# A fused two-layer graph kernel: z one step and o one step earlier, TensorE's order h, o, z, and the seventh batch's open o units done ahead of the last batch's z

## The reference, cut to what matters

```python
# layer 0: four Gaussian kernels on the relation weights, only their row sums are needed
w = exp(-0.5 * (adj[..., None] - mean) ** 2 / (1e-14 + prec ** 2))
ws = sum(w / sum(w, axis=-1), axis=2)                 # b, row, kernel
x1 = layernorm(x + concat_n(ws[n] * (x @ W[n].T)))
# layer 1: one expert per batch, chosen by the mean of x1
top1 = argmax(x1.mean(axis=1) @ router_w + router_b)
out = adj @ (x1 @ expert_w[top1])
y = relu(batchnorm_over_the_batches_of_one_expert(out))
result = layernorm(x1 + y)
```

## Time and profile before

| | us |
|---|---|
| median of 3 runs | 908.11 |
| profiled execution | 911.44 |
| its span | 909.7 |
| TensorE (PE) busy | 754.8 (83%) |
| VectorE (DVE) busy | 761.7 (84%) |
| ScalarE (ACT) busy | 772.7 (85%) |
| GpSimd (POOL) busy | 693.6 (76%) |

### The profile page before, as it was taken

How to read it: one execution, slowest core, us unless ns; L and a number is a source line. 1 busy time by engine, 2 the same in 40 slices (tenths; PEclk the granted TensorE clock), 3 DMA queues, 4 the chain that set the end, 5 groups by cost and what they waited for, 6 DMA issues and landing times.

```text
span 909.7 us, 12461 instructions
## 1 busy us (share of the span) xinstructions
PE 754.8 (83%) x3922; PEld 354.9 (39%) x3922; DVE 761.7 (84%) x1636; ACT 772.7 (85%) x761; POOL 693.6 (76%) x788
## 2 busy tenths in 40 slices
PE   1544458799999999999999999999999989994650
PEld 1211123344444444444444444444444434443640
DVE  1999988979999999999999999999999932327991
ACT  5999989989999999999999999999999811118971
POOL 6699999998888888888888888888888220002996
PEclk9866669899999999999999999999999999998895
DMA  8789887887797879877877798889766200898997
GB/s 231 206 256 254 208 225 175 211 196 197 197 239 193 190 183 239 205 190 187 232 186 187 194 243 198 194 199 234 186 163 162 47 1 0 314 359 318 333 391 284
DMA packets 262677, 191.18 MB, mean 210 GB/s; under 512 B 210002, under 2 KB 210258, under 8 KB 261074
## 3 DMA queue, kind: packets, MB, share of 16 engines
q1 hardware_dynamic: 262466, 190.38, 76.9%
q10 hardware_dynamic: 144, 0.00, 0.0%
HBM read 91.52 MB, written 48.50 MB: 154 GB/s over the span
## 4 chain that ended last, share of the span: by engine, by line
DVE 45%; POOL 22%; ACT 14%; PE 10%; issue 5%; DMA 2%; SPq 0%; DVEq 0%; POOLq 0%; ACTq 0%
DVE wgt L825 17%; DVE ps_t L857 17%; DVE x_in L844 5%; PE ps_z L1012 5%; ACT ps_t L593 4%; ACT ps_t L591 4%; POOL adj_cut L453 4%; PE ps_o L1028 3%; POOL adj_in L448 2%; POOL x_turn L464 2%; POOL x1p L490 2%; POOL adj_cut L451 2%; PE ps_t L1028 2%; POOL adjT L548 2%; DMA w_sel<-w_planes 1%
## 5 line engine op out<-in xcount | busy, mean ns | idle before, releaser
L1012 PE MATMUL ps_z<-adjT,x1p 128*128 128x512 f16 x1536 | 345.0, 381 | 0.0
L997 PE MATMUL ps_h<-w0T,x_turn 128*128 128x512 f16 x768 | 195.5, 409 | 74.0 <-DVE x_in L844 55.9
L857 DVE TENSOR_TENSOR ps_t<-ps_t,wgt 128x1024 f32<-128x1024 f32 x192 | 235.9, 1229 | 22.4 <-ACT ps_t L587 17.8
L825 DVE SCALAR_TENSOR_TENSOR wgt<-wgt,ps_t 128x1024 f32<-128x1024 f32 x192 | 224.8, 1215 | 17.4 <-ACT ps_t L593 17.2
L1012 PEld LDWEIGHTS ps_z<-adjT,x1p 128*128 128x128 f16 x1536 | 150.3, 98 | 181.6 <-issue 4.6
L576 ACT ACTIVATE wgt<-adj_in,neg_mu 128x1024 f32<-128x1024 f32 x192 | 205.8, 1136 | 8.2 <-POOL adj_in L448 8.2
L582 ACT ACTIVATE wgt<-wgt 128x3072 f32<-128x3072 f32 x64 | 176.5, 2758 | 0.0
L1028 PE MATMUL ps_o<-zT,w_sel 128*128 128x512 f16 x684 | 159.4, 383 | 6.7 <-DMA w_sel<-w_planes 6.6
L997 PEld LDWEIGHTS ps_h<-w0T,x_turn 128*128 128x128 f16 x768 | 75.8, 103 | 183.6 <-issue 95.6
L453 POOL TENSOR_TENSOR adj_cut<-adj_in,adj_cut 128x1024 f16<-128x1024 f32 x64 | 136.6, 2134 | 5.3
L1028 PEld LDWEIGHTS ps_o<-zT,w_sel 128*128 128x128 f16 x684 | 67.1, 99 | 89.8 <-DMA w_sel<-w_planes 8.5
(11 more groups left out here) (219 smaller groups left out, 859.8 us busy)
## 6 DMA issues: line engine op xcount, KB each, us to landing
adj_in<-in_adj_dram SPq DMA_DIRECT2D x64, 512.0 KB, 4.0
x_in<-in_x_dram SPq DMA_DIRECT2D x64, 256.0 KB, 4.3
x_spill<-x_in SPq DMA_DIRECT2D x28, 512.0 KB, 3.3
out_spill<-o_stage SPq DMA_DIRECT2D x49, 256.0 KB, 2.9
w_sel<-w_planes SPq DMA_DIRECT2D x8, 1024.0 KB, 5.9
adjT<-x_spill SPq DMA_DIRECT2D x6, 1024.0 KB, 12.6
out_dram<-adjT SPq DMA_DIRECT2D x6, 1024.0 KB, 7.2
adjT<-out_spill SPq DMA_DIRECT2D x4, 1024.0 KB, 13.1
```

The lines of the kernel that those rows point to most:

```text
L825: v.scalar_tensor_tensor(out=wgt[:, m % 2, j, :], in0=wgt[:, m % 2, j, :], scalar=SUM_SCALE / W0_SCALE, in1=tot, op0=ALU.mult, op1=ALU.mul ...
L857: v.tensor_tensor(tot, tot, wgt[:, n % 2, j, :], ALU.add).then_inc(dve_tot, 1)
L997: last = te.matmul(ps_h[:, n % 2, :], xT[:, n % 2, left, c, :], w0T[:, right, c, :], start=(c + i == 0), stop=(c == C - 1 and i == 2))
L1012: last = te.matmul(ps_z[:, u % 2, :], x1p[:, b % 2, left, t, k * P:(k + 1) * P], adjT[:, b % 2, right, t, half * HALF:(half + 1) * HALF], ...
```

## The change

`Z_LAG` goes from 10 to 9 and `O_LAG` from 14 to 13, so `LAST` falls from 80 to 79 and `KEPT` (from which unit on o stays on the chip) rises from 49 to 50. TensorE's step becomes h, o, z; ScalarE copies o before z. At step 65 (`FLUSH`) the four open o units of the seventh batch, 52 to 55, are all done before z(56), and at step 64 z stands ahead of o; steps 66 to 68 have no o. z(8b) waits for the x1 tiles one by one and for only the four turned tiles of adj that its half reads; the second sum for the router follows it. SyncE stores the experts' planes ahead of the transposes of steps 3, 5, 7 and 9 instead of at their ends, and the last step fetches two chunks of half a row of o instead of one.

```diff
-Z_LAG = 10
-O_LAG = 14
+Z_LAG = 9
+O_LAG = 13
...
+        FLUSH = TILES - T + Z_LAG
+        def z_unit(n):
+            return range(max(0, n - Z_LAG), min(TILES, n - Z_LAG + 1))
+        def o_units(n):
+            u = n - O_LAG
+            if n == FLUSH:
+                return range(u, TILES - T)
+            if FLUSH < n < TILES - T + O_LAG:
+                return range(0)
+            return range(max(0, u), min(TILES, u + 1))
+        def z_ahead_of_o(n):
+            return n == FLUSH - 1
...
@@ SyncE
+                if n in (3, 5, 7, 9):
+                    e = (n - 3) // 2
+                    sp.wait_ge(dve_wlo, 2 * e + 2)
+                    sp.dma_start(w_planes[e]..., planes(e)).then_inc(planes_stored, 16)
                 if n + 1 < TILES:
                     turn_adj(n + 1)
...
@@ ScalarE, step n (take_z and take_o hold the copies as before)
+                if z_ahead_of_o(n - 1):
+                    take_z(n - 1)
+                take_o(n - 1)
+                if not z_ahead_of_o(n - 1):
+                    take_z(n - 1)
                 if 0 <= n - 1 < TILES:
                     sum_reciprocal(n - 1)
...
@@ TensorE, z_product(u)
-                if u % T == 0:
-                    pe.wait_ge(pool_1l, u + T)
-                    mean(b, 1).then_inc(pe_mean, 1)
+                if k == 0:
                     for j in range(2):
-                        pe.wait_ge(adj_turned[j], 16 * (u + T) // 2)
+                        pe.wait_ge(adj_turned[j], 16 * (u + G) // 2)
                 wait(pe, dve_z, u - 1)
                 for t in range(T):
+                    if u % T == 0:
+                        pe.wait_ge(pool_1l, u + t + 1)
...
+                if u % T == 0:
+                    mean(b, 1).then_inc(pe_mean, 1)
...
@@ TensorE, step n
-                if 0 <= n - Z_LAG < TILES:
-                    z_product(n - Z_LAG)
-                if 0 <= n - O_LAG < TILES:
-                    o_product(n - O_LAG)
+                if z_ahead_of_o(n):
+                    for u in z_unit(n):
+                        z_product(u)
+                for u in o_units(n):
+                    o_product(u)
+                if not z_ahead_of_o(n):
+                    for u in z_unit(n):
+                        z_product(u)
```

More of the change, by code:

```diff
@@ L366, in fetch_o @@
                 if n == 1:
-                    sp.wait_ge(o_stored[0], KEPT // 2 * 16 + 16)
                     sp.wait_ge(dve_ws, NK * (TILES - 1))
-                    for half in (slice(0, HALF // 2), slice(HALF // 2, HALF)):
-                        sp.dma_start(o_chunk(i, 0)[:, half], out_spill[b, 0:P, half]).then_inc(o_back[i], 16)
+                    for k in range(2):
+                        sp.wait_ge(o_stored[k], KEPT // 2 * 16)
+                        sp.dma_start(o_chunk(i, k)[:, 0:HALF], out_spill[b, k * P:(k + 1) * P, 0:HALF]).then_inc(o_back[i], 16)
                 elif 1 < n < NB:
@@ L593, in sum_reciprocal, with take_z, take_o @@
                 s.activation(tot, tot, ACT.Exp, scale=-1.0).then_inc(act_rec, 1)
+            def take_z(n):
+                for u in z_unit(n):
+                    half, k = u % T // G, u % G
+                    act.wait_ge(pe_z, u + 1)
+                    if k == 0:
+                        wait(act, pe_o, u - G)
+                    if u == 0:
+                        act.wait_ge(planes_stored, 16 * E)
+                    s.activation(zT[:, 0, half, k, :], ps_z[:, u % 2, :], ACT.Copy,
+                                 scale=Z_SCALE / (ADJ_SCALE * X1_SCALE)).then_inc(act_z, 1)
+            def take_o(n):
+                for u in o_units(n):
+                    k = u % G
+                    act.wait_ge(pe_o, u + 1)
+                    if u >= KEPT:
+                        act.wait_ge(dve_ws, NK * (TILES if u // T == NB - 1 else TILES - 1))
+                        for j in range(2):
+                            act.wait_ge(adj_turned[j], 16 * TILES // 2)
+                    else:
+                        wait(act, o_stored[k % 2], u // 2 * 16)
+                        wait(act, dve_ostat, u - 1)
+                    if u == TILES - 1:
+                        act.wait_ge(dve_ostat, TILES)
+                    s.activation(out_unit(u), ps_out(u), ACT.Copy).then_inc(act_o, 1)
             for n in range(LAST):
@@ L861, in _ @@
                     y_stats(n - 2)
-                if 0 <= n - Z_LAG - 1 < TILES:
-                    low_z(n - Z_LAG - 1)
+                for u in z_unit(n - 1):
+                    low_z(u)
                 if 0 <= n - 2 < TILES:
                     y_mean_var(n - 2)
-                if 0 <= n - O_LAG - 1 < TILES:
-                    o_stats(n - O_LAG - 1)
+                for u in o_units(n - 1):
+                    o_stats(u)
                 if 1 <= n <= 2 * E:
```

33 lines of the change are left out of this document (5 added, 28 removed).

## The result

The changed kernel takes 934.79 us (median of 4 runs, 931.64 to 936.9) against 909.6 us for the kernel before on the same chip (906.81 to 911.09): ratio 1.0281, 95% interval 1.0243 to 1.0319, so it is slower. The profiled execution took 936.9 us, its span is 935.1, that is 25.4 more than before.

A forecast was written before the change was run, and what follows sets the result against it. ScalarE and VectorE were taken to bound the main part, then TensorE alone its tail. Seven delays +21.0, start +1.2 and tail -3.5 gave +18.7 us, 926.8 us on the median, range 911 to 937.

The forecast's parts named there:

- the fifth case: Rival for the whole kernel: slow landing and 2.4 us for the clock each time, +33 us, 941 us; chance 0.07.
- The wait for `w_sel` in front of z: TensorE at the first o of batches 0 to 6: seven idle times of 4 to 5 us, slow clock behind them.
- Its size: Main part, each of seven gaps: the step 3.0 us longer, 21.0 us in all; bounds for one 0.1 to 4.7.
- The landing term: Load of w_sel in the main part: lands 5.9 us after its issue (median, 4.8 to 7.0).
- The clock: TensorE's work behind each long gap runs at the slow clock, 1.8 us extra on average.
- The cause behind it: Main part: w_sel can't be asked for before the routing has chosen the expert, and only h covers its flight.
- The second case: Rival: the waits for w_sel are there but TensorE's clock stays high, +4.3 us, 912.4 us; chance 0.13.
- The third: Rival: w_sel comes in time, main part as before, the tail loses 15.5 us, 892.6 us; chance 0.09.
- The fourth: Rival: quick landings (about 5.0), gap short enough for the clock in most batches, -2 us, 906 us; chance 0.09.
- The start: First batch: ScalarE's step 10 waits for z(0), +4.7 us; the first o's stall of 3.5 goes; net +1.2.
- ScalarE's copy: Each step 8b+14: ScalarE's copy of z waits 2 to 4 us for TensorE; batch spacing grows from 88 to about 91.
- The tail: TensorE's stretch after the main part: 3.5 us shorter, no wait for x1, one of about 4 us for w_sel.

The follow-up runs named there:

- Experiment 1: The changed kernel with z ahead of o also in the step of every batch's first o: 905.82 us, ratio 0.9963 to the kernel before.
- experiment 2: The changed kernel with 18 unread matmuls on TensorE between h and the first o of batches 0 to 6: 921.05 us, ratio 1.0145 to the kernel before.
- experiment 10: The changed kernel with the old lags 10 and 14, order h, o, z and flush kept: 928.8 us, ratio 1.0233 to the kernel before.
- experiment 9: The changed kernel with old lags 10 and 14 and old order h, z, o, flush kept: 901.12 us, ratio 0.9914 to the kernel before.
- experiment 3: The changed kernel with the transpose of adj issued only after w_sel has landed, in steps that load it: 925.36 us, ratio 1.0179 to the kernel before.

## Why the prediction was right, and where it was not

The forecast was 926.8 us with a range of 911 to 937, and 934.79 was measured: slower, by the mechanism of the forecast, with 8 us more. In time it stands between the forecast and the fifth case (941), 8 us from the one and 6 from the other. By the spans it is +25.4 where the forecast had +18.7 and the fifth case +33.

**The wait for `w_sel` in front of z: right.** Seven waits of 4.01 to 5.74 us stand at the first o of batches 0 to 6 (forecast 4 to 5), with the granted clock at 0.50 to 0.70 in the 3 us behind them and o at 4.19 to 5.22 us. Experiment 1 takes z back in front at those steps alone and has all of it back.

**Its size: 4.3 us each, not 3.0.** 31.4 less 1.5 for the start is 29.9, by seven 4.3. They aren't alike: the first costs 5.4, the other six 4.1 on average, as ScalarE's waits for o and z have it (5.53 at batch 0, 3.13 to 4.83 behind it). The landing term was mis-sized: 7.8 us at the median instead of the 5.9 of the earlier trace rows, +1.9. Against it the issue came earlier, 1.17 (713.78 to 714.95) to 1.89 us behind the load of adj, 1.63 on average, where 2.37 was taken: -0.74. The clock cost 1.9, the mean of the seven o being 4.63, against 1.8; experiment 2 gives 1.8. 3.0 + 1.9 - 0.74 + 0.1 = 4.26. With means throughout (7.73 us from the issue to the o) it is 4.2, so the match is good to a tenth, not to a hundredth. The landing was taken from the kernel before, where the transpose of adj comes 3.4 us behind the load (step 54: 615.92 behind 612.52); in the changed kernel's odd step it comes 0.4 to 0.7 behind. The order rows showed the transpose (L315) next to the load, but not that it wouldn't wait.

**The cause behind it: right for this kernel, but not the whole.** The prediction gave two reasons: the load can't be asked for before the routing, which stands one step ahead of the o, and only h is left as a cover. In the changed kernel both hold, the routing ending 1.0 to 1.7 us ahead of the issue. But experiment 10 has the routing 13.4 us ahead and shows the gaps too (928.8). With the order h, o, z the place of the load in SyncE's list is enough to expose it; with z in front (experiments 1 and 9) it is covered at either lag. So the reason that decides is that the flight no longer "lay under h and z".

**The second case (clock stays high): wrong**, by the slow o and by experiment 2. **The third (faster, 892.6)** needs a `w_sel` in time; it shows up only where z covers the load, in part, in experiments 1 and 9. The fourth needed landings of about 5.0 us; the quickest of the seven o stood 6.53 us behind the issue of its load. **The fifth** was the nearest of the rivals to the result, in its landing term and not in the clock, where it took 2.4 us and 1.9 was measured.

**The start: right.** ScalarE waited for z(0) in step 10, and the reciprocal of step 10 came at 131.27 (forecast 131.0). x1's last tiles and the slow matmuls behind them:

```profile
126.59 1.46 PE L1037 MATMUL ps_z<-adjT,x1p 128*128 128x512 f16 x3 [8.31 <-POOL x1p L509]
129.28 1.46 PE L1037 MATMUL ps_z<-adjT,x1p 128*128 128x512 f16 x3 [1.23 <-POOL x1p L509]
```

```profile
130.78 0.60 ACT L622 ACTIVATE zT<-ps_z 128x512 f16<-128x512 f32 x1 [7.30 <-PE ps_z L1037]
131.27 1.02 ACT L610 ACTIVATE ps_t<-ps_t 128x1024 f32<-128x1024 f32 x1
```

Step 11 came at 142.23 instead of 137.24, +5.0 with 4.7 forecast; the stall of 3.5 at the old step of the first o went as forecast (181.02 and 191.98 are 10.96 apart). Net +1.5 against +1.2.

**ScalarE's copy: right in place, larger.** Its copy of z waited 3.13 to 4.58 us (forecast 2 to 4), in two batches behind a wait for o, and the batch spacing is 92.0 (forecast 91).

**The tail: right in sign, -5.4 for -3.5.** In TensorE's timeline there is no wait for x1, and one for `w_sel`:

```profile
761.66 2.76 PE L1055 MATMUL ps_t<-zT,w_sel 128*128 128x512 f16 x12 [1.76 <-DVE wsum L858]
...
774.62 5.34 PE L1037 MATMUL ps_z<-adjT,x1p 128*128 128x512 f16 x24
...
799.16 4.45 PE L1055 MATMUL ps_o<-zT,w_sel 128*128 128x512 f16 x12 [2.14 <-DMA w_sel<-w_planes]
...
833.51 2.76 PE L1055 MATMUL ps_o<-zT,w_sel 128*128 128x512 f16 x12 [1.42 <-DVE zT L820]
```

The forecast had 4.4 us of wait at the last batch's first o; it is 2.14, since the load, issued at 794.20, served an o at 799.16, 4.96 later and not 6.57 (why it landed sooner, no run shows). These 2.3 us are more than the whole difference of 1.9. The clock (4.45 for 2.75, 1.7) and the 1.42 us for the last low half are as forecast. The final part took 0.6 less, where nothing was counted.

**Sum.** 7 x 4.3 + 1.5 - 5.4 - 0.6 = 25.6, measured 25.4. The 4.3 was taken from the same total, so this only shows that nothing is left over; the working with 4.26 stands apart from it.

## What to carry to other kernels

In an ordered list, look at what stands between the issue of a load and its reader, and not only at how early its input is known: where both stand in the same step, the work in between is all the cover there is. Then ask what holds the issue, the input, the buffer or the place in the list; here it was the routing at the short lag and the place at the long one. When a wait is moved in front of another engine's operand, charge the stall and the clock separately, and take the flight of a load from a place where the same transfers follow it. A part of a change that fills idle time without moving a wait (here the flush, with the x1 tiles awaited one by one: 0.9% faster without the shorter lags) is worth trying without the rest.

## What the runs showed of the hardware that was not expected

- The same load of 1 MB took 5.4 to 5.9 us from issue to landing where no transpose was issued right behind it (medians of the earlier trace rows and of experiment 10), 6.4 with the transpose of adj held back (experiment 3), and 7.8 with it 0.4 to 0.7 us behind (the changed kernel). The issue of the transpose itself then holds SyncE for 5.60 to 7.83 us, against 1.93 to 2.98 in batches 0 to 5 of experiment 10, where it comes 3.4 us later. In all seven batches of the changed kernel it ends 0.16 to 0.27 us before the waiting o starts, so its length goes with the landing; which of the two holds up the other isn't shown beyond experiment 3.
- Behind an idle time of TensorE the clock doesn't go by the gap's length alone. In the changed kernel an o behind 2.14 us took 4.45, in experiment 3 one behind 2.84 took 4.39, but one behind 3.40 took 2.76 (granted clock 1.00 from 529.90 to 532.00), and before the change one behind 2.19 took 2.76. A single gap between 2 and 3.5 us can't be charged with certainty; over the seven gaps of 4.01 us and more in the changed kernel every o was slow, by 1.9 us on average.
- A wait of 3.68 us in experiment 1 for the row sums cost 1.7 more in the o behind it (4.45), so a wait that ends by an engine can cost the clock as one that ends by a DMA does.
